# One DVE copy instead of two for the transposed attention weights of heads 0 and 1 of each group of four

## What is computed

```
scores = q @ k.T * scale
p      = softmax(scores)
ctx    = p @ v
```

## Time and profile before

| | |
|---|---|
| Median of 3 runs | 1708.76 us (1704.13 to 1709.43) |
| The profiled execution's own time | 1701.59 us |
| Its span, first to last instruction | 1699.8 us |
| PE matmuls busy | 1494.0 us, 88% |
| DVE busy | 1060.7 us, 62% |
| ACT busy | 1119.1 us, 66% |
| Mean granted TensorE clock | 0.937 of full speed |

### The profile page before, as it was taken

One profiled execution on the slowest core, in us unless ns is written; L12 is line 12 of the kernel. 1 busy time (PEld: TensorE's weight loads), 2 busy tenths in 40 slices (PEclk: granted clock), 3 DMA queues, 4 the chain that ended last, 5 costly groups with the idle time before them and its releaser, 6 DMA issues.

```text
span 1699.8 us, 36608 instructions
## 1 busy us (share of the span) xinstructions
PE 1494.0 (88%) x13690; PEld 1108.7 (65%) x13690; DVE 1060.7 (62%) x2333; ACT 1119.1 (66%) x3398; POOL 64.8 (4%) x121
## 2 busy tenths in 40 slices
PE   5889949998799888999988899998899999887777
PEld 4878326666567656677766667776676776665555
DVE  2443866666477777767677767767776767675000
ACT  2442778887577788777677767677777767774111
POOL 1010000000100000000000000000000000000000
PEclk9998979999899999999999999999999999998555
DMA  9332000000322012212101211201111210100000
GB/s 336 126 115 87 0 0 1 1 1 1 112 60 79 26 51 75 64 39 76 51 27 51 76 48 55 76 26 51 51 51 51 75 52 27 51 27 1 13 16 22
DMA packets 67678, 91.24 MB, mean 54 GB/s; under 512 B 3440, under 2 KB 56688, under 8 KB 67120
## 3 DMA queue, kind: packets, MB, share of 16 engines
q1 hardware_dynamic: 67248, 88.13, 16.2%
q0 software_dynamic: 256, 0.79, 0.2%
HBM read 72.12 MB, written 16.78 MB: 52 GB/s over the span
## 4 chain that ended last, share of the span: by engine, by line
PE 63%; ACT 16%; DVE 10%; issue 10%; DMA 1%; POOL 1%; ACTq 0%; DVEq 0%; POOLq 0%
PE ps L1043 15%; PE ps L1285 10%; PE ps L1050 9%; PE ps L1311 8%; PE ps L1057 8%; PE ps L1350 4%; PE ps L1270 3%; DVE arena L986 3%; ACT dAm L501 2%; PE ps L1142 2%; DVE arena L840 2%; ACT arena L633 2%; ACT L602 1%; ACT R L685 1%; ACT arena L640 1%
## 5 line engine op out<-in xcount | busy, mean ns | idle before, releaser
L1043 PE MATMUL ps<-W,arena 128*128 128x128 f32 x2976 | 443.7, 284 | 29.2 <-ACT arena L633 15.5
L1043 PEld LDWEIGHTS ps<-W,arena 128*128 128x128 f32 x2976 | 342.0, 148 | 175.2 <-issue 131.9
L633 ACT ACTIVATE arena<-ps,nmax 128x512 f32<-128x512 f32 x640 | 434.8, 686 | 2.1 <-DVE nmax L976 1.6
L640 ACT COPY arena<-ps 128x512 f32<-128x512 f32 x320 | 187.3, 585 | 207.4 <-PE ps L1043 203.0
L976 DVE TENSOR_REDUCE nmax<-ps 128x1 f32<-128x512 f32 x320 | 206.1, 686 | 114.9 <-PE ps L1285 74.8
L986 DVE COPY arena<-ps 128x512 f32<-128x512 f32 x320 | 213.9, 687 | 50.7 <-PE ps L1043 23.0
L1285 PE MATMUL ps<-W,arena 32*128 32x512 f32 x1280 | 183.4, 640 | 30.0 <-DVE arena L986 27.5
L1311 PE MATMUL ps<-arena 128*32 128x128 f32 x5120 | 173.8, 277 | 27.9 <-ACT arena L640 27.9
L979 DVE TENSOR_REDUCE nmax<-ps 128x2 f32<-128x1024 f32 x160 | 193.7, 1211 | 0.0
L1050 PE MATMUL ps<-arena,W 128*128 128x128 f32 x1344 | 177.8, 286 | 5.7 <-ACT arena L560 5.0
L1057 PE MATMUL ps<-W,arena 128*128 128x256 f32 (+1 forms) x704 | 170.9, 382 | 4.3 <-ACT arena L596 3.6
(11 more groups left out here) (195 smaller groups left out, 1551.2 us busy)
## 6 DMA issues: line engine op xcount, KB each, us to landing
W<-keys SPq DMA_DIRECT2D x48, 512.0 KB, 3.7
arena<-values SPq DMA_DIRECT2D x48, 512.0 KB, 4.8
keys<-arena SPq DMA_DIRECT2D x16, 448.0 KB, 3.3
values<-arena SPq DMA_DIRECT2D x16, 448.0 KB, 3.9
W<-keys SPq DMA_DIRECT2D x16, 256.0 KB, 2.8
arena<-values SPq DMA_DIRECT2D x16, 256.0 KB, 3.2
W<-in_pack SPq DMA_DIRECT2D x1, 3947.0 KB, 20.3
W<-in_pack SPq DMA_DIRECT2D x1, 2246.0 KB, 10.2
```

The lines of the kernel that those rows point to most:

```text
L633: nc.scalar.activation(Pr[:, a, :], ps[:, a, :], ACT.Exp, bias=nmax[:, u % 32:u % 32 + 1], accum_out=den[:, u % 32:u % 32 + 1]).then_inc(s ...
L640: nc.scalar.copy(PT[:, (4 * Q + a) % 8, :, :].rearrange("p k n -> p (k n)"), psT).then_inc(sem("u_ev_act"), 1)
L1043: ins = nc.tensor.transpose(dst[:, k * P:(k + 1) * P], src[:, k * P:(k + 1) * P], ident)
```

## The change

The two copies that DVE makes of the turned weights of heads 0 and 1 become one instruction over both banks, 1024 columns, which waits for the turn of head 1 (`u_tp` at 4Q + 2) and stands where the copy of head 1 stood, behind the scan step 4Q+2. `u_ev_dve` now counts one for each quad, and the two waits on PE are changed to match. Places 4Q % 8 and 4Q % 8 + 1 of `PT` are neighbours, so source and target are each one run of columns.

```diff
--- before.py
+++ after.py
@@ -979,12 +979,12 @@
                 nc.vector.tensor_reduce(nmax[:, u % 32:u % 32 + 2], ps[:, 2:4, :], AX, ALU.max,
                                         negate=True).then_inc(sem("u_mx"), 1)
 
-            def keep_turned(Q, a):
-                dve.wait_ge(sem("u_tp"), 4 * Q + a + 1)
+            def keep_turned(Q):
+                dve.wait_ge(sem("u_tp"), 4 * Q + 2)
                 if Q >= 2:
                     dve.wait_ge(sem("u_pv"), Q - 1)
-                nc.vector.tensor_copy(PT[:, (4 * Q + a) % 8, :, :].rearrange("p k n -> p (k n)"),
-                                      ps[:, a, :]).then_inc(sem("u_ev_dve"), 1)
+                nc.vector.tensor_copy(PT[:, (4 * Q) % 8:(4 * Q) % 8 + 2, :, :].rearrange("p u k n -> p (u k n)"),
+                                      ps[:, 0:2, :].rearrange("p u n -> p (u n)")).then_inc(sem("u_ev_dve"), 1)
 
             def scan(i):
                 if i in SCAN_AT:
@@ -1003,11 +1003,9 @@
                     maxima(Q, 1)
                 scan(4 * Q + 1)
                 chains.at(2 * Q + 1)
-                if Q < NQ:
-                    keep_turned(Q, 0)
                 scan(4 * Q + 2)
                 if Q < NQ:
-                    keep_turned(Q, 1)
+                    keep_turned(Q)
             scan(4 * NQ + 3)
             for h in AFTER_LAST:
                 chains.at(h)
@@ -1279,7 +1277,7 @@
                     pe.wait_ge(sem(f"{l.name}_qT"), turn_side(G))
                 if Q:
                     pe.wait_ge(sem("u_exp"), 4 * Q)
-                    pe.wait_ge(sem("u_ev_dve"), 2 * Q)
+                    pe.wait_ge(sem("u_ev_dve"), Q)
                 for g in range(4):
                     rows = slice(32 * g, 32 * g + 32)
                     ins = mm(ps[:, g, :], qT[b][rows, q, :], Ks[G % 4][rows, l.key_group(q), :], start=True, stop=l is not L0)
@@ -1302,7 +1300,7 @@
                 c, li, b = STAGES[G]
                 l = LAYERS[li]
                 pe.wait_ge(sem("u_ev_act"), 2 * Q + 2)
-                pe.wait_ge(sem("u_ev_dve"), 2 * Q + 2)
+                pe.wait_ge(sem("u_ev_dve"), Q + 1)
                 if q == 0:
                     pe.wait_ge(sem(f"v_in{G % 4}"), 16 * (G // 4 + 1))
                 for kt in range(NCH):
```

## The result

The changed kernel takes 1742.05 us (median of 4 runs, 1739.99 to 1747.11) against 1706.45 us for the kernel before, measured beside it: 1.0212 times as long, 95% interval 1.0191 to 1.0234. It is 35.6 us slower. Forecast were 1755.8 us, 47 us slower, with a range from 1739 to 1777. The sign and the mechanism hold; the increment was a third too large.

The account below looks back on a forecast made before the run. The bound was taken as a loop of scores, maxima, exponentials, turns and DVE's copies, not DVE's load. Delays 28.5 + 10.3 + 11.4 = 50 us, less 3 absorbed, put +47 us on 1708.8: 1755.8 us, range 1739 to 1777.

Parts of the forecast that it names:

- The price of the copy: DVE's 1024-column copy takes 1.21 us, like the maximum over two banks; at most 2 x 687 ns = 1.37 us.
- full price: 54 quads where the scores start 0.15 us after the second copy; mean delay 0.53 us, together 28.5 us.
- second copy already late: 49 quads where DVE's own work already delays the second copy; mean delay 0.21 us, together 10.3 us.
- other release, within reach: 30 quads whose scores something else releases, but the later copy still reaches; mean 0.38 us, together 11.4 us.
- out of reach: 26 quads whose scores start well after the copies because PE was busy; no delay.
- the point of 0.56 us: A second copy starting more than 0.56 us after head 1's turn makes its quad gain instead of lose.
- ACT's backlog: ACT's queued work, a GELU with table load at times, catches up when scores start later; 3 us taken off.
- The level: Profiled execution 1701.6 us would become 1748.6; the same 47 us put on the median of 1708.8 gives 1755.8.
- The dear copy: Rival: DVE's copy takes 1.37 us, 133 quads lose 0.16 us more; +68 us, 1777 us; chance 0.06.
- The absorbed case: Rival: PE's waits ahead of other lines shrink by half of the scores' loss; +24 us, 1733 us; chance 0.07.
- The faster case: Rival: scores wait for DVE's accumulated work, so its 26 us less shortens the span; 1683 us; chance 0.03.
- The two rules of the Trainium skill: Larger operations help a saturated engine; splitting helps where unsaturated Scalar or Vector cause bubbles elsewhere. The forecast sided with the second.

Follow-up runs that it names:

- Experiments 2: Changed kernel with its one copy cut to half the columns of each bank from the third quad on; 1682.43 us, 0.9854 of the kernel before.
- experiment 3: Changed kernel plus one tiny DVE copy per quad ahead of the maxima of heads 0 and 1; 1743.96 us, 1.0223 of the kernel before.
- the first experiment: Kernel before with head 0's copy moved behind scan step 4Q+2, still two copies; 1736.9 us, 1.0174; repeated 1738.63 us.
- two_waiting: Two copies behind scan step 4Q+2, both waiting for head 1's turn, against the two moved copies without that wait; 1757.78 us, 1.0293.

## Why the prediction was right, and where its size was off

**The bottleneck.** Right. It had the scores' wait for DVE's copy as the link of the loop, and DVE's own load as irrelevant. Experiments 2 and 3 show both. That load was mis-sized, though: DVE's busy time fell by 16 us on the page and that of the copies by 19 (213.9 to 194.5), not by 26, since two copies in a row take 1.29 us together and not 2 x 0.69. It had been costed at nothing, so the sum did not suffer.

**The price of the copy.** Right: 1.223 us against 1.21. The upper bound of 1.37 us was not reached even by two copies (1.29).

**The four kinds of quads.** I took the time from the end of head 1's turn to the next scores in both traces, quad by quad:

| kind | quads | forecast us | measured us |
|---|---|---|---|
| full price | 54 | 28.5 | 26.9 |
| second copy already late | 49 | 10.3 | 9.1 |
| other release, within reach | 30 | 11.4 | 10.8 |
| out of reach | 26 | 0 | 0.0 |
| sum | 159 | 50.2 | 46.7 |

The smallest distance of 0.15 us behind the copy now occurs in 134 quads, before in 103; "some 130" were forecast. The term that was mis-sized is the start of the copy where a chain piece of DVE precedes it. There I charged the scan step with its full 0.15 us and the way from ACT to DVE. Behind a busy DVE a scan step holds back the next start by only some 0.07 us, and in the quad of 1202.9 us, for instance, the scores came 0.09 us earlier after the turn than before, where I had them 0.07 us later. For the same reason the point of 0.56 us, from which a late second copy was to make the change a gain, is not a good rule. Of the 26 quads beyond it 17 gained, but only 0.05 to 0.09 us, and 8 lost 0.29 to 0.51 us: a second copy that is late because DVE was busy or its scan step waited leaves the one copy little or no earlier start.

**Absorbed.** I took 3 us off for ACT's backlog. The rest of the quad, from the scores to head 1's turn, is 4.6 us shorter in total, but not for that reason: 3.2 us of it are two quads in which the kernel before ran at half clock and the changed one did not (below). The backlog gave back next to nothing.

**The level.** In the profiled executions the change costs 40.5 us: 46.7 - 4.6 = 42.1 us in the stage, and 1.6 us come back outside it. The medians are 35.6 us apart. The 5 us between the two are where the profiled executions lie among the runs: that of the kernel before took 1701.6 us, 5 below its median of 1706.45, that of the changed kernel 1742.11, on its median. This goes with the clock. In the 28 runs of the kernel before that stand beside the experiments, those with a mean granted clock of 0.937 or 0.938 took 1700 to 1702 us, as the profiled one with 0.937 did, and those with 0.931 or 0.932 took 1707 to 1711. All nine runs of the changed kernel had 0.939 to 0.943. Putting the 7 us between the profile and the median of the kernel before on the changed kernel as well was 5 us too much. So of the 11 us by which the increment was too high, 5 are the stage's 42.1 against 47, some 2 are outside the stage, and 5 lie between profile and medians.

**The rivals.** The dear copy is out by 1.223 us. The absorbed case had the waits of the earlier trace rows ahead of other lines shrink by 26 us; they shrank by 5 (27.9 to 26.1, 17.0 to 15.8, 6.9 to 4.9). The faster case is out by experiment 3. The two rules of the Trainium skill ("Perfetto Trace Analysis", "Optimizing Scalar/DVE Operations") that were set against each other: with the one on unsaturated engines that cause bubbles, the runs agree. The rule on larger operations isn't false here either, though it speaks of a saturated engine and DVE is busy for 60%: the one instruction saved 13 us against two with the same wait, 8.5 of them in the wait itself.

What I had not separated at all is the move from the merge. I priced them together, which gave nearly the right sum, and the first experiment missed because it needed the parts.

## What to carry to other kernels

When two instructions become one, the one carries the later of their two waits for all its data: ask what the first did while the second's input was being made, and price the time from the last input to the signal, not the engine's busy time. Read it in the timeline of single quads, and count the kinds. At an engine that is busy for 62% and ends PE's idle time 79 times, fewer and larger instructions are no gain for their own sake; whether still smaller ones would be, no run here shows. And before moving work into a gap, look which other wait it covers where it stands.

## What was not expected of the hardware

Kernels that differ in DVE's copies alone differ in how often PE drops to half clock. The same stretch of one quad in the kernel before and in the changed kernel, each with two of PE's groups of matmuls that follow (columns of the stretches as in the earlier trace rows; the scores start at 981.80 and at 1003.00):

```profile
980.00:984.00 4.00, 2.20 (x18) 1.39 (x19) 3.11 (x10) 1.28 (x4) 0.09 (x1) 0.94 0.01 2
984.00:986.00 2.00, 2.00 (x14) 1.67 (x17) 1.97 (x4) 1.84 (x5) 0.00 (x0) 0.50 0.00 0
```

```profile
983.66 1.92 PE L1050 MATMUL ps<-arena,W 128*128 128x128 f32 x8
...
985.93 1.53 PE L1311 MATMUL ps<-arena 128*32 128x128 f32 x32
```

```profile
1001.20:1005.20 4.00, 2.20 (x20) 1.39 (x21) 3.14 (x8) 1.45 (x4) 0.14 (x1) 1.00 0.00 0
1005.20:1007.20 2.00, 2.00 (x42) 1.64 (x42) 1.97 (x4) 1.79 (x6) 0.00 (x0) 1.00 0.00 0
```

```profile
1004.79 1.06 PE L1048 MATMUL ps<-arena,W 128*128 128x128 f32 x8
...
1005.99 1.08 PE L1309 MATMUL ps<-arena 128*32 128x128 f32 x32
```

In both PE is busy for 2.20 of the first 4 us. Before, the granted clock fell to 0.50 within them (0.94 in the mean), the 1.2 GHz level, and a group of 8 matmuls took 1.92 us; after, it stayed at 1.00, the 2.4 GHz level, and the same 8 took 1.06 us. By the clock records of the traces, the stage ran 20 us at half clock in the kernel before, 14 in the changed one (17 in its second profile), 44 and 51 in the two profiles of the moved copies, 37.5 in two_waiting. The same matmuls of the stage cost 1022 us of PE time before, 1017 in both profiles of the changed kernel, and 1032.5 in the kernel with two moved copies:

```profile
443.00:1594.00 1151.00, 1032.52 (x11444) 769.69 (x11437) 796.35 (x1781) 827.07 (x2486) 31.92 (x58) 0.98 0.16 50
```

That is 15 us between two kernels, against an effect of 36 us that is studied here. In the profiles, where the move costs 41 us (spans 1699.8 and 1740.9), the time from head 1's turn to the scores grew by 33 us, which is the wait, and PE's busy time in the stage by another 10 us. Its runs show the same: three with a granted clock of 0.937 or 0.938 took 1732 to 1735 us, three with 0.928 to 0.930 took 1743 to 1745. So a median of few runs can be off by some 5 us with the clock alone, and the waits in the trace tell such terms apart better. What decides whether a short gap in PE's work costs a drop was not tested.
